# Second-layer attention scores as one rounded pass over stacked high and low rows, with sliced query and value weights

## Time and profile before

| | us |
|---|---|
| median of 3 runs (4319.76 to 4323.09) | 4321.95 |
| the profiled execution, its own time | 4322.45 |
| its span in the trace | 4320.2 |
| TensorE busy | 4034.8 (93%) |
| ScalarE busy | 2828.5 (65%) |
| VectorE busy | 2522.5 (58%) |
| GpSimd busy | 1106.3 (26%) |

### The profile page before, as it was taken

How to read it: one execution, slowest core, us unless ns; L and a number is a source line. 1 busy time by engine, 2 the same in 40 slices (tenths; PEclk the granted TensorE clock), 3 DMA queues, 4 the chain that set the end, 5 groups by cost and what they waited for, 6 DMA issues and landing times. The chain is left out here.

```text
span 4320.2 us, 88382 instructions
## 1 busy us (share of the span) xinstructions
PE 4034.8 (93%) x31232; PEld 3487.0 (81%) x31232; DVE 2522.5 (58%) x8076; ACT 2828.5 (65%) x8373; POOL 1106.3 (26%) x1335
## 2 busy tenths in 40 slices
PE   0899999999999999999999999999999999999998
PEld 0787888888788888888888788887888888888886
DVE  3446565565656556565565656556565565656555
ACT  2666676666667666676666667666676666667663
POOL 0222222222222222222222222222222222222212
PEclk9999999999999999999999999999999999999996
DMA  4000000000000000000000000000000000000000
GB/s 126 3 3 7 3 7 4 4 7 4 5 5 7 4 4 8 3 7 4 5 7 4 5 5 7 4 4 7 3 7 5 4 7 4 5 5 5 4 2 4
DMA packets 34047, 34.41 MB, mean 8 GB/s; under 512 B 4336, under 2 KB 31824, under 8 KB 33616
## 3 DMA queue, kind: packets, MB, share of 16 engines
q1 hardware_dynamic: 26752, 25.47, 2.1%
q10 hardware_dynamic: 6864, 3.30, 0.4%
HBM read 23.52 MB, written 5.24 MB: 7 GB/s over the span
## 5 line engine op out<-in xcount | busy, mean ns | idle before, releaser
L1053 POOL TENSOR_TENSOR SE<-SE,rs 128x512 f32<-128x512 f32 (+1 forms) x640 | 557.6, 871 | 2228.5 <-DVE rs L926 2228.5
L719 ACT ACTIVATE SE<-PS,mx 128x128 f32<-128x128 f32 (+2 forms) x3840 | 979.3, 343 | 186.8 <-DVE qq L950 113.1
L705 ACT ACTIVATE PTs<-PT 77x512 f32<-77x512 f32 (+2 forms) x960 | 574.0, 598 | 79.7 <-PE PT L601 64.1
L664 ACT ACTIVATE qk<-PG 128x256 f32<-128x256 f32 x640 | 247.8, 387 | 560.1 <-PE PG L446 314.7
L921 DVE TENSOR_REDUCE sums<-SE 128x4 f32<-128x512 f32 (+1 forms) x640 | 365.3, 571 | 423.1 <-ACT SE L719 422.9
L601 PE MATMUL PT<-ident,SE 128*128 128x128 f32 (+2 forms) x3840 | 596.7, 279 | 8.0 <-POOL SE L1053 7.9
L577 PE MATMUL PS<-qk 128*128 128x154 f32 (+1 forms) x2560 | 590.6, 353 | 7.3 <-ACT qk L666 5.7
L910 DVE TENSOR_REDUCE mx<-PS 128x4 f32<-128x308 f32 (+2 forms) x960 | 501.0, 522 | 109.3 <-PE PS L577 92.0
L601 PEld LDWEIGHTS PT<-ident,SE 128*128 128x128 f32 (+2 forms) x3840 | 451.9, 146 | 69.8 <-issue 41.1
L1045 POOL TENSOR_TENSOR n<-qq,p_half 128x4 f32<-128x4 f32 x320 | 323.4, 1011 | 713.2 <-DVE qq L950 713.2
L561 PE MATMUL PW<-w_o,OTs 128*128 128x160 f32 x2560 | 462.4, 304 | 9.7 <-ACT OTs L697 9.6
(11 more groups left out here) (203 smaller groups left out, 7669.5 us busy)
## 6 DMA issues: line engine op xcount, KB each, us to landing
xres<-in_x_dram SPq DMA_DIRECT2D x32, 160.0 KB, 2.4
out_dram<-x SPq DMA_DIRECT2D x64, 80.0 KB, 1.6
shared<-in_ctx_dram SPq DMA_DIRECT2D x32, 154.0 KB
w_o<-in_L_xattn_a_wo_dram ACTq DMA_DIRECT2D x2, 800.0 KB, 11.3
SE<-in_L_xattn_a_wq_dram SPq DMA_DIRECT2D x2, 640.0 KB, 4.8
qk<-in_L_xattn_a_wq_dram SPq DMA_DIRECT2D x8, 160.0 KB, 4.7
SE<-in_L_xattn_a_wk_dram SPq DMA_DIRECT2D x2, 640.0 KB, 4.1
SE<-in_L_xattn_a_wv_dram SPq DMA_DIRECT2D x2, 640.0 KB, 3.9
```

Of the source, the lines that this page charges most:

```text
L705: a_(PTs[0:J, place % 2, :], PT[0:J, :], ACT.Copy).then_inc(S["pts_done"], 1)
L719: last = a_(SE[:, place % 4, J * i:J * i + J], PS[place % 2][:, step * i:step * i + J], ACT.Exp, bias=mx[:, place % 2, i:i + 1])
L1053: gp.tensor_tensor(e, e, rs[:, n % 2, :].unsqueeze(2).to_broadcast([128, 4, J]), ALU.mult)\
```

## The change

- `scores` for layer 1: queries and keys are each split into a rounded high part and a low remainder. Three copies of the 32 rows are stacked into 96 rows: queries as high, low, high (`q1st`), keys as high, high, low (`k1st`). One `float32r` matmul with 96 contraction rows and 308 columns replaces the float32 one with 32 rows.
- The split: ACT writes the high part from PSUM (`q1_hi`, `k1_hi`), DVE then the remainder (`q1_lo`, `k1_lo`). SP copies the rows into the stacks by SBUF-to-SBUF DMAs: 15 per `q1` job (5 row sets of 32, three copies) and 15 for the keys of a group, in the slot after the job. Each unit's 3 copies of the queries have a semaphore of their own.
- `k1` handles all four batches at once: two jobs per group in place of four, at slots 54 and 57, each with 328 context columns.
- The block-diagonal keys are made per unit by GpSimd (`own_keys`, 96x308), two slots ahead of the unit, ahead of `normalise` in the slot, into one of three buffers. DVE's expansion in `k1` is gone.
- `a1_wq` and `a2_wv` no longer stay in SBUF. Setup writes their split forms to DRAM; in the pipeline SP loads per l0 self-attention unit a slice of 128 columns in three parts (192 KB), and per context value job a slice of 256 columns in four parts (512 KB), each into one of two buffers, as soon as the job two before has been done.
- In setup the pieces are in another order, two of the staging targets are shared temporaries, and ACT waits for the copies to DRAM before it writes a temporary again.
- SP's loop over the groups becomes a walk over the slots: slices, stores, contexts, x, stacks.
- On TensorE the `v` jobs move from the slot's end to between the transposes and `wo`.

```diff
-    K1_SLOT = {0: (54, 57), 1: (77, 78)}
-    LAST_K1_SLOT = {0: (54, 57), 1: (74, 75)}
+    K1_SLOT = (54, 57)
...
+        q0_slice = sb("q0_slice", [128, 2, 3, 128], f32r)
+        q0_split = nc.dram_tensor("q0_split", [NP, 128, 3, 128], fp32, kind="Internal").ap()
...
-        w_vc = sb("w_vc", [128, 2, 2, INNER], f32r)
+        vc_slice = sb("vc_slice", [128, 2, 2, 2, 256], f32r)
+        vc_split = nc.dram_tensor("vc_split", [NP // 2, 128, 2, 2, 256], fp32, kind="Internal").ap()
...
+                        for dst, src in SPLITS[i - 2][4]:
+                            sp.dma_start(dst, src.bitcast(fp32)).then_inc(copied, 16)
...
+                    if out_copies and copies:
+                        act.wait_ge(copied, 16 * copies)
...
+        slices_at = slots((JOB_SLOT[NAME_OF[(kind, i - 2)]] + 1 if i >= 2 else FIRST, (kind, i)) for kind, i in NAME_OF)
...
+        stacks_at = slots([(STEP * g + Q1_SLOT[h] + 1, ("q1", g, h)) for g in range(GROUPS) for h in range(2)]
+                          + [(STEP * g + K1_SLOT[1] + 1, ("k1", g, 1)) for g in range(GROUPS)])
...
+                def load_slice(kind, i):
+                    if i >= 2:
+                        sp.wait_ge(S["job_full"], JOB[NAME_OF[(kind, i - 2)]] + 1)
...
+                for t in range(FIRST, LAST):
+                    for kind, i in slices_at(t):
+                        load_slice(kind, i)
+                    for g, b, d in tails_at(t):
+                        if d == 8:
+                            store(g, b)
+                    for g, h in contexts_at(t):
+                        load_context(g, h)
+                    for g, h in xs_at(t):
+                        load_x(g, h)
+                    for kind, g, h in stacks_at(t):
+                        if kind == "q1":
+                            sp.wait_ge(S["q1_done"], 2 * g + h + 1)
...
+                            for w in range(W1):
+                                r, row = (0, 32 * w) if w < 4 else (1, 96)
+                                for k, src in enumerate((q1_hi, q1_lo, q1_hi)):
+                                    sp.dma_start(q1st[32 * k:32 * k + 32, h, w, :].bitcast(fp32), src[row:row + 32, r, :].bitcast(fp32))\
+                                        .then_inc(S[f"q1_in{h}{w}"], 16)
...
-                        if w == 0 and b % HB == 0:
-                            pe.wait_ge(S["q1_done"], NTH[("q1", g, h)])
-                            pe.wait_ge(S["kbd_done"], NTH[("k1", g, 1, h)])
-                        r, row = (0, 32 * w) if w < 4 else (1, 96)
-                        last = mm(ps[:, 0:4 * T], q1T[row:row + 32, h, r, 128 * (b % HB):128 * (b % HB) + 128],
-                                  kbd[row:row + 32, r, b % HB, :, :].rearrange("p h t -> p (h t)"),
-                                  start=True, stop=True)
+                        if b % HB == 0:
+                            pe.wait_ge(S[f"q1_in{h}{w}"], 16 * 3 * (g + 1))
+                        pe.wait_ge(S["kbd_done"], l1_count(g, n))
+                        last = mm(ps[:, 0:4 * T], q1st[:, h, w, 128 * (b % HB):128 * (b % HB) + 128],
+                                  kbd[:, l1_count(g, n) % 3, :, :].rearrange("p h t -> p (h t)"), start=True, stop=True)
...
                     if t - PT_LAG in UNIT_AT:
                         probs_transposed(UNIT_AT[t - PT_LAG])
+                    for name in late_at(t):
+                        if name[0] == "v":
+                            job(name)
...
+                    elif kind == "q1":
+                        ps = take(name)
+                        dve.wait_ge(S["q1_hi"], 2 * g + i + 1)
+                        v.scalar_tensor_tensor(q1_lo[:, :, :].rearrange("p r n -> p (r n)"), ps[:, :], SCALE1,
+                                               q1_hi[:, :, :].rearrange("p r n -> p (r n)").bitcast(fp32),
+                                               ALU.mult, ALU.subtract).then_inc(S["q1_done"], 1)
...
+                def own_keys(g, k):
+
+                    b, w, j = k // W1, k % W1, l1_count(g, k)
+                    if k == 0:
+                        pool.wait_ge(S["k1_in"], 16 * 3 * W1 * (g + 1))
+                    if j > 3:
+                        pool.wait_ge(S["s_done"], PLACE[("l1",) + divmod(j - 4, GB * W1)] + 1)
+                    gp.tensor_tensor(kbd[:, j % 3, :, :], k1st[:, w, b, :].unsqueeze(1).to_broadcast([96, 4, T]),
+                                     head_of_row[0:96, :].unsqueeze(2).to_broadcast([96, 4, T]), ALU.mult)\
+                        .then_inc(S["kbd_done"], 1)
```

More of the change, by code:

```diff
@@ L164, in xattn_program @@
-        for name, tile in (("L0_xattn_a2_wk", w_kc), ("L0_xattn_a2_wv", w_vc),
-                           ("L1_xattn_W_k", w_k1), ("L1_xattn_W_v", w_v1)):
+        w = D["L0_xattn_a1_wq"]
+        copy = lambda dst, src: (dst.rearrange("p k n -> k p n"), src.rearrange("k (p n) -> k p n", p=NP))
+        SPLITS.append(([(w[0:128, :], 0, 128)], TEMP[0], TEMP[1], INNER,
+                       [copy(q0_split[:, :, 0, :], TEMP[0]), copy(q0_split[:, :, 1, :], TEMP[1])]))
+        for name, tiles in (("L0_xattn_a1_wk", w_k0),):
+            n = D[name].shape[1]
+            SPLITS.append(([(D[name][0:128, :], 0, 128)], tiles[0][:, :], tiles[1][:, :], n, []))
+            SPLITS.append(([(D[name][128:C, :], M * r, M * r + M) for r in range(4)], tiles[2][:, :], None, n, []))
@@ new lines, in xattn_program @@
+        SPLITS.append(([(w[128:C, :], M * r, M * r + M) for r in range(4)], TEMP[0], None, INNER,
+                       [copy(q0_split[:, :, 2, :], TEMP[0])]))
+        w = D["L0_xattn_a2_wv"]
+        copy = lambda dst, src: (dst.rearrange("p k n -> k p n"), src.rearrange("k (p n) -> k p n", p=NP // 2))
+        SPLITS.append(([(w[0:128, :], 0, 128)], TEMP[0], TEMP[1], INNER,
+                       [copy(vc_split[:, :, 0, 0, :], TEMP[0]), copy(vc_split[:, :, 0, 1, :], TEMP[1])]))
+        for name, tiles in (("L0_xattn_a1_wv", w_v0),):
+            n = D[name].shape[1]
+            SPLITS.append(([(D[name][0:128, :], 0, 128)], tiles[0][:, :], tiles[1][:, :], n, []))
+            SPLITS.append(([(D[name][128:C, :], M * r, M * r + M) for r in range(4)], tiles[2][:, :], None, n, []))
@@ new lines, in xattn_program @@
+        w = D["L0_xattn_a2_wv"]
+        copy = lambda dst, src: (dst.rearrange("p k n -> k p n"), src.rearrange("k (p n) -> k p n", p=NP // 2))
+        SPLITS.append(([(w[128:256, :], 0, 128)], TEMP[0], TEMP[1], INNER,
+                       [copy(vc_split[:, :, 1, 0, :], TEMP[0]), copy(vc_split[:, :, 1, 1, :], TEMP[1])]))
+        for name, tiles in (("L0_xattn_a2_wq", w_q1_0),):
+            n = D[name].shape[1]
+            SPLITS.append(([(D[name][0:128, :], 0, 128)], tiles[0][:, :], tiles[1][:, :], n, []))
+            SPLITS.append(([(D[name][128:C, :], M * r, M * r + M) for r in range(4)], tiles[2][:, :], None, n, []))
@@ L340, in xattn_program @@
             NTH[name] = seen[name[0]] = seen.get(name[0], 0) + 1
+        SLICE = {}
+        for name in JOBS:
+            for kind, own in SLICED:
+                if own(name):
+                    SLICE[name] = (kind, sum(1 for x in SLICE.values() if x[0] == kind))
+        NAME_OF = {x: name for name, x in SLICE.items()}
+        JOB_SLOT = {name: t for t in range(FIRST, LAST) for name in qk_at(t) + late_at(t)}
+        slices_at = slots((JOB_SLOT[NAME_OF[(kind, i - 2)]] + 1 if i >= 2 else FIRST, (kind, i)) for kind, i in NAME_OF)
         def read_out(name):
             freed_by = {"xT": "nT_dve", "qk": "qk_done", "v": "v_done", "cT": "cT_dve", "ff": "h_done",
-                        "down": "down_added", "q1": "q1_done", "k1": "kbd_done", "vip": "vip_done",
+                        "down": "down_added", "q1": "q1_done", "k1": "k1_done", "vip": "vip_done",
                         "ctx1": "gv_done", "ipT": "ipT_done", "ip": "o1_done", "oT1": "o1T_done", "y": "y_done"}
@@ L486, in job @@
                                 pe.wait_ge(S["cT_dve"], 2 * g + h + 1)
[L487 removed]
+                        if a == 0:
+                            s = slice_in(name)
+                            rows160(ps[:, 0:HT], [q0_slice[:, s, j, :] for j in range(3)], 0, h)
+                        else:
+                            rows160(ps[:, 0:HT], w_q1_0, 128 * p, h)
                         if a == 0:
```

164 lines of the change are left out of this document (99 added, 65 removed).

## The result

The changed kernel takes **4442.44 us** (median of 4 runs, 4427.54 to 4451.93) against 4322.49 for the kernel before: a ratio of 1.0271, 95% interval 1.0234 to 1.0308. The forecast was 4214 us. The profiled execution has a span of 4443.8 us, 123.6 more than before, and a mean granted clock of 0.949, against 0.981.

The account below looks back on a forecast made before the run. TensorE, busy 93% of the span, was taken to set the pace in most slots. 4322.45 - 163 (scores) - 21 (keys) - 8 (values' job) + 54 (hand-over) + 8 (clock) + 22 (start) = 4214 us; range 4130 to 4305.

Parts of the forecast that it names:

- Step 1: Layer-1 scores on TensorE: one matmul of 0.14 us saves 0.66 us a unit, 218 us in all, 163 reaching the end.
- Three quarters of it reach the end: Five waits per group swallow the saving of 5 of 20 units, so 0.75 of the 218 us comes off.
- Rival C: ScalarE and VectorE take over in the mixed slots, only 40% of the saving comes through: 4303 us; chance 0.13.
- Step 2: Key jobs on TensorE: 32 jobs of 1.32 us replace 64 of 1.11, 29 us saved, 21 of it counted.
- Step 3: VectorE, ScalarE, GpSimd: GpSimd's added key expansions, at most 224 us, lie in its idle time; cost 0.
- Step 4: Values' job earlier on TensorE gives ScalarE more time before `wo`: 8 us off, ends 0 and 25.
- Step 5: Weight slice loads on SyncE's queue stay hidden, tight behind the 15 key DMAs: cost 0, end 16 us.
- Step 6: Query hand-over before a group's first scores: TensorE waits 3.4 us more per group, 54 us, ends 40 and 75.
- Step 7: TensorE's clock after the hand-over's stop: 8 us lost, ends 0 and 27.
- Rival D: The queries' hand-over pulls the clock down in slots 62 to 66 of each group: slower, 4366 us; chance 0.06.
- E: Rival: the score pass is shortened but slices or stacks come late, time comes out near 4322 us; chance 0.05.
- Step 8: Start: copies to DRAM and x behind four slices cost 22 us, ends 8 and 40; first norm near 115 us.

Follow-up runs that it names:

- e3: The changed kernel with both cuts: weight slices loaded only twice, first-half query stack built only for the first group; 4267.16 us, ratio 0.9885.
- e2: The changed kernel without the first half's query stack copies, and TensorE's wait for them, after the first group; 4379.53 us, ratio 1.0148.
- e1: The changed kernel with only the first two slices of each kind of query and value weights loaded; 4337.66 us, ratio 1.0044.
- e4: The kernel before with its 32-row score matmul in the rounded type, remainders left out, no stacks or slices; 4278.78 us, ratio 0.9913.
- e13: e12 with e4's rounded 32-row score matmul, remainders left out; 4226.35 us, ratio 0.9788.
- e12: The kernel before with values' jobs early on TensorE and VectorE copying the values right after the slot's maxima; 4236.97 us, ratio 0.9819.
- e8: The kernel before with VectorE's product and sum for the l1 output norm cut to 8 of 73 columns; 4272.34 us, ratio 0.9908.
- e9: e4 with VectorE's product and sum for the l1 output norm cut to 8 of 73 columns; 4233.73 us, ratio 0.981.
- e10: e6 with the values' jobs back at the end of TensorE's slot; 4335.26 us, ratio 1.0056.
- e6: e5 with a group's first layer-1 units moved from slots 4 and 5 to 6 and 9, and x loaded before the first slices; 4308.48 us, ratio 0.9977.
- e7: The changed kernel with 38 idle matmuls before TensorE's wait for each group's first query stack; 4380.51 us, ratio 1.0138.
- e5: The changed kernel with stack DMAs spread over slots, a row set at a time, behind each slot's slices; 4334.79 us, ratio 1.0036.
- e14: e13 with three idle matmuls before each layer-1 score matmul of the first 15 groups; 4255.47 us, ratio 0.9844.
- e11: e6 with VectorE copying the values out right after the slot's maxima; 4209.74 us, ratio 0.9764.

## Why the prediction was wrong

The forecast's own sum, put into the ledger's terms: work -247 (218 and 29), clock +8, and the rest of the -108, +131, for idle time (54 for the hand-over, 22 at the start, a quarter of the saving, less 8). Measured: -213, +131, +206. So of the 232 us by which the span was missed, 34 are work, 75 idle time and 123 the clock. The 75 are the slices' waits (74.4): what the other waits took is near what the forecast allowed them.

The runs split the miss of the time, 228 us, in another way. Without its terms for the hand-over and the clock the forecast is 4152 us; e3, without both stops, takes 4267. So 115 us belong to a saving that doesn't come through, and 113 to the stops, which cost 175 us and were forecast at 62. Of the stops, the hand-over with its clock was nearly right in sum (63 us, e2); the slices, at 105 us (e1), were forecast at nothing. Steps 1, 5 and 7 failed.

**Step 1, the scores: size a sixth too large, its reach wrong.** The timeline of TensorE after, a new score matmul and its successor:

```profile
2053.46 0.41 PE L684 MATMUL PS<-kbd,q1st 96*128 96x308 f32 x1
2053.71 0.28 PE L517 MATMUL PG<-nT,q_slice 128*128 128x256 f32 x1
```

0.25 us to the next start, not 0.14; nothing is exposed ahead of it. That is the other end that step 1 gave (0.11 behind), and 0.55 saved per unit: 176 us instead of 211. The prediction had named score matmuls 0.25 us apart as a sign of being wrong.

"Three quarters of it reach the end" was the failing part: e4 lets through 44 of 122 us, e13 against e12 11 of 112. Five waits per group were counted as five places that swallow what stands just ahead of them. But in e4 nothing at all is gained in slots 4 to 24, and the waits that grew (values' copy, norm, `normalise`) say that these slots already had the length of a loop through other engines, with TensorE only a few tenths of a microsecond from waiting: shorten its work there and it waits. Which engine's loop it is was not taken apart; e8 and e9 only show that VectorE's norm product is not it.

The stretch with 79.47 of 80 us busy is also not pure layer-0, as the prediction has it. `L586` in that stretch of the kernel before:

```profile
L586 PE MATMUL PS<-kbd,q1T x10: 417/470/522, 1754.9 to 1816.2; 32*128 32x308 f32 x10
```

Five pairs of score matmuls lie in it, those of the thinly set slots 37 to 53, and the forecast carried it over to the crowded slots, where twelve units stand in 21 slots. Rival C had that mechanism with 40%, and was put at 0.13.

**Step 2, the keys: right.** The new job takes 0.99 us for its six matmuls and 0.36 for the image part, 1.35 (forecast 1.32).

**Step 3, GpSimd: nearly right.** Its product takes 703 ns on average, 224 us as forecast, but TensorE does wait for it: 17.5 us in 17 waits.

**Step 4, the values' job: another wait, and a larger gain.** Forecast 8, its upper end 25; e10 says 27 (34 by ratios). The wait that the 8 us were taken from, `wo` for ScalarE, is the same with the late job (16.0 us in e10) and the early one (15.9 in e6). What shrinks is the query job's wait for the values' copy, from 75.9 to 58.9 us, which the prediction had only in its upper end.

**Step 5, the slices: the step that failed outright.** It found the right place, behind the key DMAs, and priced it at nothing. Timeline of SyncE's queue and TensorE after, at slot 59 to 61:

```profile
1919.85 6.21 SPq L504 DMA_DIRECT2D k1st<-k_hi  x10
1926.10 4.50 SPq L504 DMA_DIRECT2D k1st<-k_lo  x5
1930.64 0.58 SPq L475 DMA_DIRECT2D q_slice<-q_split  x1
...
1933.37 0.36 PE L517 MATMUL PG<-nT,q_slice 128*128 128x256 f32 x1 [3.52 <-DMA q_slice<-q_split]
```

15 DMAs take the queue 10.8 us, not 6.8. The row used was that of four loads from DRAM (0.46 each); these move 32 rows from SBUF to SBUF and take 0.62 us back to back (1.22 for two). Four microseconds more on a margin of "within a microsecond" is the wait of 3.5. The second half's 15 DMAs were declared harmless since its queries have nine slots; they hold the queue from 2001.75 to 2012.16, and a slice stands behind them: the same wait again, which makes 30. What was late was not the transfer but the next one in the queue.

**Step 6, the hand-over: right.** 64.5 us more of waiting (forecast 54, ends 40 and 75), 3.84 per group instead of 3.4.

**Step 7, the clock: mechanism named, size and premise wrong.** "8 us; ends 0 and 27" became 131. Its upper end took only a half-clock stretch as long as the stop. Rival D gave the deciding point as 14.5 us of half clock per group; the changed kernel has 18 more per group than before (457 less 171, over 16), and D's time was 4366. D was right that the stop pulls the clock down (e2, e7), and E that slices come late (e1, e5). What neither had is that both happen in the same kernel, and that the clock falls without any long stop too (e13, e14).

D's chance of 0.06 rested on "the body holds 1.00". That was read from one stretch of 80 us, and it isn't so: in the kernel before 79 of the 171 us at half clock lie in the body, and its mean granted clock of 0.981 could have told. Two stretches of the kernel before, the first with no wait of TensorE longer than 0.9 us:

```profile
1725.80:1731.80 6.00, 4.78 (x39) 3.96 (x39) 3.52 (x11) 2.21 (x5) 1.04 (x1) 1.00 0.00 0
1731.80:1735.20 3.40, 3.40 (x15) 2.99 (x13) 2.55 (x10) 1.92 (x8) 0.14 (x1) 0.51 0.00 0
```

So the clock was already falling behind short waits, in slots 22 to 32, and in the changed kernel 198 of the body's 369 us at half clock begin there.

By the Trainium skill ("TensorE: Matmul & The Clock Gate", HAM oscillation — how this bites in real kernels) idle gaps between bursts of matmuls bring the half rate. The trace agrees, in the stretches around 1952. The Trainium skill (the same page, A second HAM failure mode: psum-queue depth-cycling) has a kernel in which many short pauses do so too. The trace agrees here as well, in e13's stretches around 1601.

**Step 8, the start: about right.** The first norm starts at 111.14 (forecast "near 115"), the first scores 17.9 us later than before (forecast 22).

**What stays open.** How the loss splits between idle time and clock in a single slot wasn't taken apart. Nor was it shown why e6, without the stops, keeps 351 us at half clock when e3 has 233. No run had the exact changed kernel with both faults of the stop mended and nothing else moved; e6 comes nearest. e12's stacked counterpart e11 is the fastest run of the study; whether still later first units would take the rest of its half-clock time (219 us) wasn't tried.

## What to carry to other kernels

A busy share near 93% doesn't make TensorE the bound of each slot: ask of every slot which loop sets its length, and count a saving in full only where TensorE doesn't wait at all, as in the last group here. A stretch is evidence for its own slots only. Cost a new DMA by what it does to the queue it shares, with a row of its own kind, and look for the transfer that comes next in line. And before TensorE's work is shortened, or a stop put in, look for half-clock stretches in the kernel as it is and ask what the clock will do: the same stop with TensorE kept busy was 62 us cheaper, and the best change of this study was not a shorter matmul but one copy moved forward on VectorE.

## What the runs showed of the hardware that I had not expected

- The clock falls without any long stop: in e13 a stretch at 0.51 stands behind 6 us in which TensorE was busy for 4.89, with single waits of 1.1 us at most, and in the kernel before one stands behind 6 us with 4.78 busy. Half-clock time went 122, 231, 102 us from e12 over e13 to e14, as work was taken out and put back.
- Idle matmuls can make a kernel faster: 608 of them took 62 us off (e7).
- A 32-row float32r matmul over 308 columns takes 0.33 us to the next start (e4), a 96-row one 0.25 with the same columns.
- A DMA of 32 rows within SBUF takes SyncE's queue 0.62 us in the changed kernel, a load of a weight piece from DRAM 0.43 to 0.46 in the kernel before.
